# Product-key stages of a transformer block: token-half products, two groups of y keys, a later normaliser

## The reference

```
x = x + 0.5 * L0_ffn(layernorm(x))       # per-feature small MLP
x = x + L0_attn(layernorm(x))            # 64-token windows, 16 heads of 8
x = x + 0.5 * L0_ffn(layernorm(x))
x = x + 0.5 * product_keys(layernorm(x))
x = x + L1_attn(layernorm(x))            # top-u queries per head
x = x + 0.5 * product_keys(layernorm(x))
```

```
xn  = batchnorm(x)                                     # over all 4096 tokens
q   = xn @ w_q.T                                       # 2 sides x 8 heads x 128
sim = q . keys                                         # 2 sides x 8 heads x 32 keys
sx, sy = top8(sim x side), top8(sim y side)
scores, idx = top8(sx[:, None] + sy[None, :])          # expert = 32 * x key + y key
o = gelu(x . key_in[idx]) * softmax(scores)
out = sum over heads and picks of o * key_out[idx]
```

## Time and profile before

| | |
|---|---|
| median of three runs | 1385.57 us (1384.21 to 1385.87) |
| the profiled execution | 1384.7 us, its span 1382.8 us |
| granted TensorE clock, mean | 0.933 of full speed |
| TensorE matmul busy | 1149.3 us (83%) |
| TensorE weight load busy | 943.9 us (68%) |
| VectorE busy | 1099.3 us (79%) |
| ScalarE busy | 915.0 us (66%) |
| GpSimd busy | 722.3 us (52%) |

### The profile page before, as it was taken

The page is one execution under the profiler, slowest core; times in us unless marked ns, Lnnn a source line. Parts: engine busy times, 40 slices in busy tenths (PEclk is TensorE's granted clock), DMA queues, the critical chain, the costliest instruction groups (busy, mean ns, idle before and its releaser), DMA issues.

```text
span 1382.8 us, 57023 instructions
## 1 busy us (share of the span) xinstructions
PE 1149.3 (83%) x22892; PEld 943.9 (68%) x22892; DVE 1099.3 (79%) x3996; ACT 915.0 (66%) x2135; POOL 722.3 (52%) x645
## 2 busy tenths in 40 slices
PE   2756899876748899999998679999569999999986
PEld 1643666655627888888888357777348888888886
DVE  4955888857789898999894568888598989889870
ACT  3853666647657778778784446666468788787881
POOL 4234544413047777878775500000167788787872
PEclk9976999978959999999999879999769999999999
DMA  6000000000002222222222000000012222222222
GB/s 162 17 0 1 1 0 0 1 1 1 1 6 59 48 46 46 46 46 60 47 46 50 1 1 1 0 0 1 0 32 50 46 46 48 54 51 46 46 63 78
DMA packets 27542, 43.10 MB, mean 31 GB/s; under 512 B 6960, under 2 KB 18480, under 8 KB 27440
## 3 DMA queue, kind: packets, MB, share of 16 engines
q1 hardware_dynamic: 27440, 41.82, 13.5%
HBM read 6.15 MB, written 2.10 MB: 6 GB/s over the span
## 4 chain that ended last, share of the span: by engine, by line
PE 48%; DVE 16%; ACT 11%; issue 9%; POOL 6%; DMA 5%; SPq 4%; ACTq 0%; POOLq 0%; DVEq 0%
PE bank L1760 15%; PE bank L1742 5%; POOL work L346 5%; DMA rowsD<-work 5%; ACT work L1072 4%; DVE work L907 3%; SPq L316 3%; PE bank L1468 3%; PE bank L1733 3%; ACT L1231 2%; PE bank L1644 2%; DVE work L949 2%; PE bank L1481 2%; PE bank L1626 2%; PE bank L1365 2%
## 5 line engine op out<-in xcount | busy, mean ns | idle before, releaser
L1760 PEld LDWEIGHTS bank<-rowsD,work 128*32 128x32 f32 x16384 | 359.8, 194 | 85.1 <-issue 84.5
L1760 PE MATMUL bank<-rowsD,work 128*32 128x32 f32 x16384 | 370.4, 275 | 50.0 <-DMA rowsD<-work 31.2
L421 POOL TENSOR_SCALAR work<-work 128x1024 f32<-128x1024 f32 x64 | 185.9, 2904 | 126.7 <-ACT work L1236 126.7
L408 POOL TENSOR_TENSOR work<-work 128x512 f32<-128x512 f32 x128 | 161.2, 1281 | 41.8 <-ACT work L1264 29.7
L1264 ACT ACTIVATE work<-bank 128x512 f32<-128x512 f32 x128 | 74.9, 611 | 151.4 <-PE bank L1760 148.0
L1236 ACT ACTIVATE work<-work 128x128 f32<-128x128 f32 x512 | 160.5, 402 | 4.1 <-DVE work L969 4.1
L1245 ACT ACTIVATE work<-work 128x128 f32<-128x128 f32 x512 | 162.0, 413 | 0.0
L423 POOL TENSOR_TENSOR work<-work 128x1024 f32<-128x1024 f32 x64 | 157.0, 2453 | 5.3
L949 DVE STREAM_TRANSPOSE work<-work 128x1024 f32<-128x1024 f32 x128 | 151.3, 1221 | 0.0
L1771 PE MATMUL bank<-kout,work 128*128 128x128 f32 x1024 | 128.1, 278 | 3.0 <-POOL work L408 3.0
L1742 PE MATMUL bank<-xT,kinT 128*128 (+1 forms) x512 | 126.9, 393 | 2.6 <-ACT work L1255 2.6
(11 more groups left out here) (193 smaller groups left out, 2285.4 us busy)
## 6 DMA issues: line engine op xcount, KB each, us to landing
rowsD<-work SPq DMA_DIRECT2D x256, 128.0 KB, 2.4
x_sb<-in_L_attn_x_dram SPq DMA_DIRECT2D x8, 256.0 KB, 4.9
out_dram<-x_sb SPq DMA_DIRECT2D x4, 512.0 KB, 5.4
headsel<-in_c_headsel_dram SPq DMA_DIRECT2D x1, 512.0 KB, 4.5
work<-in_L_ffn_key_in_dram SPq DMA_DIRECT2D x1, 512.0 KB, 8.1
kout<-in_L_ffn_key_out_dram SPq DMA_DIRECT2D x4, 128.0 KB, 5.1
work<-in_L_ffn_keys_dram SPq DMA_DIRECT2D x1, 256.0 KB, 3.0
wqkv<-in_L_attn_W_qkv_dram SPq DMA_DIRECT2D x1, 192.0 KB, 4.3
```

The source lines that it names most:

```text
L408: last = nc.gpsimd.tensor_tensor(cg[:, par, :].rearrange("p (j t) -> p j t", j=NCH)[:, :, half * 64:half * 64 + 64], csb[:, par, 512 * hal ...
L421: nc.gpsimd.tensor_scalar(wmask, both, 1.0 - 5e-7, None, ALU.is_ge).then_inc(s["wm"], 1)
L1760: last = nc.tensor.matmul(bank[2 + half][k * NK:(k + 1) * NK, :] .rearrange("p (j t c) -> p t c j", j=NCH, t=16)[:, t % 16, :, :], xrows[: ...
```

## The change

`KH` is 2 groups of y keys with `NJY` = 16 keys each, in place of 4 groups with 8. The 128 partitions of the expert side are now (side, group, x key): side is the half of the tile's tokens.

- `products`: 32 quads x 2 groups = 64 matmuls a tile with 64 moving columns (4 tokens x 16 y keys) in place of 128 with 32. A half takes 8 quads of each side, so the four partition quarters are still taken in turn.
- `outputs`: 16 y keys x 2 sides = 32 matmuls a tile, each on 64 partitions of input and 64 of output, in place of 8 on all 128.
- `experts`: a unit is 4 y keys x 2 sides = 8 matmuls with 64 weight columns and 128 tokens, in place of 2 with 128 and 256. It reads `xs5`, which holds four tiles, instead of `xT`; GpSimd's copy into `xs5` waits for `experts` of the pair before instead of the last `zT`.
- The Gelu, the combine and the weight layouts `kinT` and `kout` follow; `kout` is loaded twice, once for each side.
- TensorE's loop body holds two pairs (6 iterations, pairs 1 to 12); pairs 0, 13, 14 and 15 are unrolled.
- VectorE: the softmax's sum and reciprocal (`normaliser`) move from the end of `back` to after the next tile's `front`.
- `xmask` is laid out head by head, so that it reads the bank in order; `xrest` likewise, and L969 reads it turned.
- `headsel` is loaded and kept cut to what is used.

```
 def products(n, par, pair):
-    yrows = rowsD[...].rearrange("p c (k j t) -> p k t c j", k=4, t=32)
+    yrows = rowsD[...].rearrange("p c (k j t) -> p k t c j", k=KH, t=32)
-        for t in range(16 * half, 16 * half + 16):
-            for k in range(4):
-                matmul(bank[2 + half][k * NK:(k + 1) * NK, :]..., xrows[:, t, :], yrows[:, k, t, :, :])
+        for t in range(8):
+            for side in range(2):
+                quad = 16 * side + 8 * half + t
+                for k in range(KH):
+                    q = KH * side + k
+                    matmul(bank[2 + half][q * NK:(q + 1) * NK, :]..., xrows[:, quad, :], yrows[:, k, quad, :, :])

 def outputs(m, par):
-    for j in range(NCH):
-        matmul(bank[6][:, par * D:(par + 1) * D], cg[:, par, j * P:(j + 1) * P], kout[:, j, :])
+    for j in range(NJY):
+        for side in range(2):
+            r = slice(side * 64, (side + 1) * 64)
+            matmul(bank[6][r, par * D:(par + 1) * D], cg[r, par, j * 64:(j + 1) * 64], kout[r, j, :])

-def experts(p, u):
-    for j in range(2):
-        matmul(bank[4 + u % 2][:, j * 2 * P:(j + 1) * 2 * P], kinT[:, 2 * u + j, :, :], xT[:, bass.ds(p * 2 * P, 2 * P)])
+def experts(p, pp, u):
+    pair = xs5[:, 2 * pp:2 * pp + 2, :].rearrange("p x (s t) -> p s x t", s=2)
+    for j in range(4):
+        for side in range(2):
+            matmul(bank[4 + u % 2][side * 64:(side + 1) * 64, j * P:(j + 1) * P], kinT[:, 4 * u + j, :, :], pair[:, side, :, :])

-with pe.Fori(1, NPAIR - 2) as p:
-    sequence(p)
+with pe.Fori(0, NPAIR // 2 - 2) as i:
+    sequence(2 * i + 1, 1)
+    sequence(2 * i + 2, 0)
+sequence(NPAIR - 3, 1)

 # VectorE
-tensor_tensor(xmask, keyed(par, 0), top8[:, par, 0:PH, 1].unsqueeze(1).to_broadcast([P, NK, PH]), is_ge)
+xs = bank[par][:, 0:PH * NK].rearrange("p (h k) -> p h k", h=PH)
+tensor_tensor(xmask, xs, top8[:, par, 0:PH, 1].unsqueeze(2).to_broadcast([P, PH, NK]), is_ge)
 def tile(i, par, ahead=True, done=True):
     if ahead:
         front(i + 2, par)
+    if not (isinstance(i, int) and i == NT - 1):
+        normaliser(i + 1, 1 - par)
     turn(i, par)
     if ahead:
         back(i + 2, par)
     if done:
         update(i - 2, par)
```

More of the change, by code:

```diff
@@ L23 @@
 NCH = NE // P
+KH = 2
+NJY = NK // KH
 LN_EPS = 1e-5
@@ L53, in build @@
         vmask = sb("vmask", [P, 2])
-        headsel = sb("headsel", [P, 8, P])
+        headsel = sb("headsel", [P, 2, NK])
         stats = sb("stats", [P, NT, 6])
@@ L211, in build @@
         o += o % 2
-        xs5, o = cut(o, P)
+        xs5, o = cut(o, 4, P)
         zT, o = cut(o, 2, P)
@@ L218, in build @@
         eq1 = bank[7][:, 192:208]
-        xrest = bank[7][:, 256:512].rearrange("p (k h) -> p k h", h=PH)
+        xrest = bank[7][:, 256:512].rearrange("p (h k) -> p h k", h=PH)
         cz, o = cut(o, 2, PH, 8)
@@ L224, in build @@
         rz, o = cut(o, 2, PH)
-        xmask, o = cut(o, NK, PH)
+        xmask, o = cut(o, PH, NK)
         rows5, o = cut(o, 2, 4, 512)
@@ L228, in build @@
         rowsT, o = cut(o, 2, 2, NE)
-        G5, o = cut(o, 2, 4, NCH, P // 2)
+        G5, o = cut(o, 2, 4, NJY, NK)
         cg, o = cut(o, 2, NE)
@@ L293, in _ @@
             load(vmask[:, :], A["c_vmask"])
-            load(headsel[:, :, :], A["c_headsel"])
+            load(headsel[:, :, :], A["c_headsel"][:, 0:2, 0:NK])
             load(wqkv[:, :], A["L0_attn_W_qkv"])
@@ L423, in threshold, with tile @@
                     nc.gpsimd.tensor_tensor(both, both, wmask, ALU.mult).then_inc(s["W"], 1)
-                def tile(n, par, gpar, ahead=True):
+                def tile(n, par, gpar, pair=0, slot=0, ahead=True):
                     threshold(n, par)
@@ L994, in tile @@
                         update(i - 2, par)
-                for n in range(2):
-                    front(n, n)
-                    back(n, n)
+                front(0, 0)
+                back(0, 0)
+                front(1, 1)
+                normaliser(0, 0)
+                back(1, 1)
                 tile(0, 0, done=False)
@@ L1347, in head_norms @@
                     for g in range(4):
-                        last = nc.tensor.matmul(bank[2 + half][32 * g:32 * (g + 1), 0:SEQ], headsel[:, odd, 0:32],
+                        last = nc.tensor.matmul(bank[2 + half][32 * g:32 * (g + 1), 0:SEQ], headsel[:, odd, :],
                                                 squares[half][:, 2 * g + odd, :], start=(odd == 0), stop=(odd == 1))
@@ L1740, in experts @@
                     pe.sem_inc(s_go, 1)
-                    for j in range(2):
[L1742 to L1745, removed]
+                    pair = xs5[:, 2 * pp:2 * pp + 2, :].rearrange("p x (s t) -> p s x t", s=2)
+                    for j in range(4):
+                        for side in range(2):
+                            last = nc.tensor.matmul(bank[4 + u % 2][side * 64:(side + 1) * 64, j * P:(j + 1) * P],
+                                                    kinT[:, 4 * u + j, :, :].rearrange("p k i -> p (k i)"),
+                                                    pair[:, side, :, :], start=True, stop=True)
                     last.then_inc(s["o"], 1)
@@ L1769, in outputs, with sequence @@
                     pe.sem_inc(s_go, 1)
-                    for j in range(NCH):
-                        last = nc.tensor.matmul(bank[6][:, par * D:(par + 1) * D],
-                                                cg[:, par, j * P:(j + 1) * P],
-                                                kout[:, j, :], start=(j == 0), stop=(j == NCH - 1))
+                    for j in range(NJY):
+                        for side in range(2):
+                            r = slice(side * 64, (side + 1) * 64)
+                            last = nc.tensor.matmul(bank[6][r, par * D:(par + 1) * D], cg[r, par, j * 64:(j + 1) * 64],
+                                                    kout[r, j, :], start=(j == 0), stop=(j == NJY - 1))
                     last.then_inc(s["y"], 1)
-                def sequence(p, before=True, ahead=2):
+                def sequence(p, pp, before=True, ahead=2):
                     if before:
```

76 lines of the change are left out of this document (38 added, 38 removed).

## The result

The changed kernel takes 1413.83 us (median of four runs, 1410.53 to 1415.52), the kernel before 1385.1 beside it: a ratio of 1.0211, 95% interval 1.0187 to 1.0235. It is 29 us slower. The forecast was 1356 with a range up to 1406; rival A of the prediction, with 1404, is what happened, only dearer.

The account below looks back on a forecast made before the run. No engine was taken as full; a ring of waits through all engines bound the kernel. A pair falls from 22.06 to 20.99 us, 28 us in 26 pairs, plus 2 elsewhere: 1384.7 less 30, plus 0.9, told as 1356; range 1328 to 1406.

Parts of the forecast that it names:

- rival A: TensorE's loop body: grown to 1808 loads and matmuls, it isn't kept and its code is refetched; +49 us, 1404; chance 0.27.
- The sum that gave 1356: Whole kernel: a pair falls from 22.06 to 20.99 us in 26 pairs, 28 us, plus 2 at the ends: 30 off.
- 22 ns was issue: Products: issue, not columns, sets the matmul's pace, so 64 columns cost what 32 do: 22.05 ns, 2.82 us a tile.
- Rival C: Products: the strided read sets the pace, 44 ns a matmul, so nothing is gained; about 1490 us; chance 0.06.
- Outputs: TensorE's outputs: 64 instructions a tile at 63.75 ns, 4.08 us in place of 1.89.
- B: TensorE's outputs: both sides' matmuls share a bank and don't overlap, 118 ns each, 7.55 us a tile; 1535; chance 0.07.
- TensorE's sum: TensorE's work a pair: products 5.64, outputs 8.16, experts 4.08 and similarities 1.94 make 19.82 us for 20.45.
- The ring through Exp: Waits through all engines, with VectorE's sum waiting for ScalarE's Exp, close the old 22.06 us pair; the later normaliser cuts it.
- the ring that I had counted (20.99): Odd tile, turn to turn: copies, products, similarity, experts, outputs, update, front, sum and reciprocal, turn; 20.99 us.
- A sign read wrongly: VectorE before update: waiting for outputs by more than a microsecond was listed as showing the forecast wrong.
- long done: GpSimd's copy into xs5: the experts two pairs back, for which it now waits, would have finished long before; no cost.

## Why the prediction was wrong, point by point

- **The step that failed** is the treatment of the loop body. The forecast's sum has no term for it; the prediction had the body's growth, the fetch of blocks and the point from which it decides, as rival A, but gave it 0.27, "against: the largest body so far shows none". A body of 4.6 blocks that is kept says nothing of one of 7.3. With the term taken away the kernel takes 1356.65 us (one pair in the body) or 1360.18 (no loop), so the failed step is worth 54 to 57 us. Even A was too cheap: it put 3.72 us on a return, the time of one block. The stop alone is near that, 3.2 on the mean; but behind it the granted clock falls to 0.50 in eight returns of ten and the outputs take 1.5 us longer on the mean, and by the whole times a return costs 5.4. Inside the body A put 12 us; the unrolled version takes 3.5 more than the one-pair body, within the spread.
- **The sum that gave 1356** was partly lucky. It took the gain of a pair from the one pair of the earlier trace rows, 22.06 to 20.99, 1.07 us; but the mean of twelve pairs is 21.57, from which 20.99 is only 0.58 away, 15 us in 26 pairs and not 28. The one-pair kernel gains 0.72 a pair in stage 5 and 0.67 in stage 3 (22.01 to 21.34), 18 us in 26 pairs; the other 9 come at the starts and ends of the stages, for which the sum had 2.
- **Products** were mis-sized: 2.82 us a tile forecast, 3.67 measured. From two clocks I had concluded that 22 ns was issue. That they hardly follow the clock was right; that what remains must be issue was not. Read in order, the new ones take 17.9 ns and do follow it, so for them it is the strided read. Rival C, where it sets the pace in full (44 ns), overstated it.
- **Outputs** were mis-sized the other way: 4.08 forecast, 3.64 measured (1163.97 to 1167.61), 57 ns each; experts 0.95 us a unit for 1.02. Two tiles of the array at different rows and columns, writing different partitions of one bank, do overlap: two of them take 114 ns, less than the 118 of one matmul of the old outputs with as many columns. B is out, and the rule of the Trainium skill, "TensorEngine Tiling (Array Packing)", "Restrictions and Gotchas", that different row tiles can't access one bank at the same time doesn't bite here.
- **TensorE's sum** is 2 x (3.67 + 3.64) + 4 x 0.95 + 2 x 1.05 = 20.5 us a pair, forecast 19.82, before 20.45. That the products' halving goes back into outputs was right, more so than forecast. The two errors, 0.85 us too little and 0.44 too much a tile, cancel in part.
- **VectorE**: L911 at 415 ns as forecast (0.31 us off). The prediction left open whether the order of keys or the strided threshold had cost it. L937, whose order of keys changed as well, took 427 ns before and 426 after, which speaks for the threshold; no run parts the two. The ring through Exp bound the kernel before, and its cut was worth 1.3%, the mask 0.9%; together they give on the old TensorE program all that the whole change was forecast to give. For TensorE's new program the later normaliser costs 9.5 us. Its 0.37 us stand in the ring that I had counted (20.99) and would not in the old place, 10 us in 26 pairs; that this is the whole reason is argued, not shown, and in full the difference is 6 us and within the spread (1360.18 and 1354.13). I hadn't asked whether the ring through Exp still binds once products are short. It doesn't: 2.5 us of waits for 23.3.
- **A sign read wrongly**: VectorE waiting for outputs before update by more than a microsecond was to speak against the forecast. It does wait so (1.69 us at 1160.57, one pair in the body), and had to: with 19.3 us of work in a pair of 20.99 it must stand somewhere, once Exp no longer holds it.
- **The rest** cost what was forecast: L410, the combine, takes 1298 ns for 1281, and L971, which reads `xrest` turned, 679 for 681. GpSimd's copy into `xs5` waits, by the kernel's own count, for the experts two pairs back, as the prediction has it. They are not "long done": with one pair in the body it waits for them 33.0 us in 10 waits from 1060 to 1280 us. But GpSimd is not the bound, and no other engine shows a wait on the copy.

## What to carry to other kernels

Count the instructions of a loop body whenever a change unrolls it by two: here one of 6.3 blocks of 256 was kept and one of 7.3 fetched anew, at about 5 us a return, while straight code cost hardly anything. A stop of TensorE can cost more than itself, as its clock may be lower after it. A resource that shows no trace of itself at today's size is an open cost, not a free one. Take a change apart before judging it, and don't expect the parts to add up: here the two parts on VectorE give 2.0% alone, TensorE's part and the mask 2.7% (with one pair in the body), and all three 2.1%. The later normaliser and the shorter products loosen the same ring, so one of them is enough.

## What the runs showed of the hardware

- A loop body of TensorE with 1552 weight loads and matmuls (and some 60 other instructions) ran without a packet of code, one of 1808 was fetched anew in each iteration; the stop at the return was 3.2 us on the mean of ten.
- After such a stop the granted clock was 0.50 for some microseconds in eight of ten cases, and 64 matmuls of 64x64 tiles then took 5.0 to 6.6 us for 3.71.
- A product matmul with 32 weight columns and 64 moving ones in four column groups starts every 17.9 ns if the moving elements stand in a row, every 28.7 if they stand 128 bytes apart, at the granted clock 1.00. With the clock at 0.50 for most of the tile it is 26 and 28.8. The order of the write to the bank made no difference (one run).
- A transpose of 1024 elements a partition in 32x32 blocks takes 1.22 us with a write in order and 1.98 us with elements 128 bytes apart.
- 64x64 tiles on the array's diagonal with 128 moving columns, writing one bank, start every 57 ns.
- A compare over 256 elements takes 415 ns when the other operand is held over 32 elements and 727 when it changes with each, 32 bytes apart (the order of the first operand changed with it).
